# Attention tokens routed in two sets into a fixed region per expert, with slots read through a table

## What is computed

```python
t = rmsnorm(x) * rms_w
q, k, v = t @ wq, t @ wk, t @ wv                     # 8 heads of 64
attn = softmax(causal(q @ k.T * scale))
x = layernorm(x + (attn @ v * sigmoid(t @ w_gates)) @ wo)
logits = x @ Wg                                      # 16 experts
topi = top_k(logits, 2); gates = softmax over the two chosen
y = sum over the chosen e of gates[e] * ((silu(x @ W1[e] + b1[e]) * (x @ W11[e] + b11[e])) @ W2[e] + b2[e])
z = silu(x @ Ws1 + bs1) * (x @ Ws11 + bs11) @ Ws2 + bs2
out = layernorm(x + y + z)
```

## Time and profile before

| what | value |
|---|---|
| median of 3 runs | 682.15 us (680.07 to 682.47) |
| the profiled execution, its own time | 682.44 us |
| its span | 679.3 us |
| mean granted clock of TensorE | 0.965 |
| TensorE busy | 619.2 us (91%) |
| VectorE busy | 484.1 us (71%) |
| ScalarE busy | 418.7 us (62%) |
| GpSimd busy | 121.3 us (18%) |
| attention's last sum ends | 510.97 us |
| scatters run | 529.72 to 573.6 us |
| slots' matmuls start | 577.78 us |

### The profile page before, as it was taken

One profiled execution on the slowest core, in us unless ns is written; L12 is line 12 of the kernel. 1 busy time (PEld: TensorE's weight loads), 2 busy tenths in 40 slices (PEclk: granted clock), 3 DMA queues, 4 the chain that ended last, 5 costly groups with the idle time before them and its releaser, 6 DMA issues.

```text
span 679.3 us, 14812 instructions
## 1 busy us (share of the span) xinstructions
PE 619.2 (91%) x5300; PEld 509.4 (75%) x5300; DVE 484.1 (71%) x1564; ACT 418.7 (62%) x909; POOL 121.3 (18%) x243
## 2 busy tenths in 40 slices
PE   4899999999999999999999999999968898999930
PEld 2678888858888886888888688888856366999930
DVE  3788767688877677877767797776788533668736
ACT  4786556687666568765656877556664211677746
POOL 4000000002000000000000000000000676688830
PEclk9899999999999999999999999999987899899985
DMA  6520000050000005000000498000067211333242
GB/s 139 118 55 1 1 2 1 2 125 1 1 2 1 1 2 116 10 1 1 3 1 1 94 194 27 1 1 2 1 200 175 37 48 55 83 90 89 79 127 85
DMA packets 56504, 33.57 MB, mean 49 GB/s; under 512 B 23920, under 2 KB 49776, under 8 KB 56432
## 3 DMA queue, kind: packets, MB, share of 16 engines
q1 hardware_dynamic: 53872, 27.38, 19.5%
q0 software_dynamic: 2560, 5.26, 2.3%
HBM read 14.75 MB, written 9.48 MB: 36 GB/s over the span
## 4 chain that ended last, share of the span: by engine, by line
PE 68%; DVE 10%; POOL 10%; issue 6%; DMA 2%; ACT 2%; SPq 1%; DVEq 0%; POOLq 0%; ACTq 0%
PE ps_o L1079 19%; PE ps_t L966 18%; PE ps_s L1048 12%; PE ps_s L1050 10%; POOL x_sorted L466 5%; PE ps_o L1089 4%; POOL y_rows L482 4%; DVE k_l L672 3%; DVE q_hl L672 2%; PE ps_s L1199 2%; POOL row_all L473 1%; PE ps_s L974 1%; ACT k_h L501 1%; PE ps_o L1187 1%; DVE bn L707 1%
## 5 line engine op out<-in xcount | busy, mean ns | idle before, releaser
L966 PE MATMUL ps_t<-ident,probs 128*128 128x128 f32 x1104 | 173.7, 275 | 12.0 <-ACT probs L513 11.9
L966 PEld LDWEIGHTS ps_t<-ident,probs 128*128 128x128 f32 x1104 | 135.1, 141 | 48.8 <-issue 11.6
L544 ACT ACTIVATE probs<-probs,nmax 128x128 f32<-128x128 f32 (+15 forms) x128 | 153.6, 1200 | 21.2 <-DVE nmax L775 12.3
L784 DVE COPY probsT<-ps_t 128x512 f32<-128x512 f32 (+3 forms) x160 | 91.2, 570 | 101.4 <-PE ps_t L966 100.4
L555 ACT ACTIVATE probsT<-ps_t 128x512 f32<-128x512 f32 (+3 forms) x160 | 89.6, 560 | 98.7 <-PE ps_t L966 97.3
L1048 PE MATMUL ps_s<-k_h,q_hl 128*128 128x512 f32 (+3 forms) x320 | 142.3, 448 | 0.5 <-DMA k_l<-k_l 0.5
L1079 PE MATMUL ps_o<-probsT,v_sb 128*64 128x128 f32 x2176 | 140.0, 277 | 1.3 <-DVE x_acc L799 1.2
L1079 PEld LDWEIGHTS ps_o<-probsT,v_sb 128*64 128x64 f32 x2176 | 116.8, 137 | 19.6 <-issue 14.6
L770 DVE TENSOR_SCALAR_CACHE_REDUCE probs<-ps_s 128x512 f32<-128x512 f32 x192 | 128.4, 686 | 0.7
L1050 PE MATMUL ps_s<-k_l,q_hl 128*128 128x512 f32 (+3 forms) x320 | 117.0, 366 | 0.0
L438 POOL TENSOR_TENSOR rden<-rsum,gate 128x2 f32<-128x2 f32 x64 | 12.5, 195 | 402.6 <-ACT probs L544 387.4
(11 more groups left out here) (148 smaller groups left out, 706.2 us busy)
## 6 DMA issues: line engine op xcount, KB each, us to landing
k_h<-k_h SPq DMA_DIRECT2D x32, 128.0 KB, 2.3
k_l<-k_l SPq DMA_DIRECT2D x32, 128.0 KB, 2.4
w_all<-in_L_ffn_W SPq DMA_DIRECT2D x2, 2048.0 KB, 11.0
xg<-x_sorted SPq DMA_DIRECT2D x48, 64.5 KB
x_sorted<-zeros SPq DMA_DIRECT2D x12, 256.0 KB, 8.5
act_s<-y_rows SPq DMA_DIRECT2D x8, 256.0 KB, 4.8
x_acc<-in_L_attn_tokens SPq DMA_DIRECT2D x4, 256.0 KB, 3.8
out<-x_acc SPq DMA_DIRECT2D x4, 256.0 KB, 2.3
```

Of the source, the lines that this page charges most:

```text
L544: nc.scalar.activation(probs[s % 2][h][:, 0:w], probs[s % 2][h][:, 0:w], ACT.Exp, bias=nmax[:, row], scale=-1.0, accum_out=rsum[:, row]).t ...
L784: nc.vector.tensor_copy(probsT[s % 2][h][:, c * BT:c * BT + w // P, :].rearrange("p n i -> p (n i)"), ps_t[1][:, 0:w]).then_inc(moved1, 1)
L966: return nc.tensor.transpose(dst, src, ident[:, :])
```

## The change

Tokens are routed in two sets: set 0 is tiles 8 to 15 (n0, n1), set 1 is tiles 0 to 7. Each expert has a fixed region of 2048 rows in x_sorted, so that a token's row is the expert's region plus its rank, and set 0 needs no counts of set 1. x_sorted grows from 6144 to 34816 rows. A table of first rows, one for each slot tile, is made on VectorE, and SyncE reads it into registers. The end of attention has an order written out for each engine, statistics of n0 and n1 move to steps 10 and 11, the square root goes to GpSimd as a power of -0.5, gates come from tanh in place of an exponential, and the routing, norms and gates of the sets are laid between the steps of the shared expert. Tiles in SBUF are placed in another order, so that the first norms can be written while attention still runs. The cast of slot numbers moves from GpSimd to VectorE.

```diff
-    norm_at = {NT: [("stats", n0), ("stats", n1)], NT + 1: [("norm", n0), ("norm", n1), ("stats", n2)]}
+    SETS = (range(n1 * BT, (n0 + 1) * BT), range(n3 * BT, (n2 + 1) * BT))
...
+    PE_UNITS = [pair_units(False, {}),
+                ending(pair_units(True, {}),
+                       [t14a, wo12, pv13, t14b, t15a, wo13, t15b, pv14, pv15, unit("turn_x", c=n0), wo14, wo15,
+                        unit("turn_x", c=n1)])]
+    ACT_UNITS = [pair_units(False, ACT_LAG),
+                 ending(pair_units(True, ACT_LAG),
+                        [wo12, pv13, t14b, t15a, wo13, pv14, t15b, wo14, pv15, wo15, unit("turn_x", c=n0),
+                         unit("turn_x", c=n1)])]
+    DVE_UNITS = [pair_units(False, DVE_LAG),
+                 ending(ahead(ahead(pair_units(True, DVE_LAG), unit("times_wo", 10), unit("stats", c=n0)),
+                              unit("times_wo", 11), unit("stats", c=n1)),
+                        [wo12, unit("norm", c=n0), t14b, pv14, wo13, t15a, t15b, pv15, unit("norm", c=n1),
+                         unit("stats", c=n2), wo14, wo15])]
...
+            def empty_groups(groups):
+                for g in groups:
+                    sp.dma_start(view[g, :, :, 0:D], zeros[:, :].rearrange("p (n d) -> p n d", d=D)).then_inc(zfill, 16)
+
+            empty_groups(range(groups // 2))
             for p in range(PAIRS - 1):
                 for x in PE_UNITS[0]:
                     if x[:2] == ("project", K):
                         k_across(x, p * KQ_FILLS + (KQ_FILLS + high_of[x]),
                                  p * FREED + (KQ_FILLS + fill_of[x] + ONE))
-
-            sp.wait_ge(zero_set, 2)
-            view = x_sorted.rearrange("(g n p) d -> g p n d", p=P, n=BT)
-            for g in range(SLOT_TILES // BT):
-                sp.dma_start(view[g, :, :, 0:D], zeros[:, :].rearrange("p (n d) -> p n d", d=D)).then_inc(zfill, 16)
-            with nc.allow_non_contiguous_dma("one number of each row, 24 KB"):
-                sp.dma_start(x_sorted.rearrange("(n p) d -> p n d", p=P)[:, :, D].bitcast(i32),
-                             empty_row[:, :]).then_inc(zfill, 16)
+                if p == 0:
+                    empty_groups(range(groups // 2, groups))
+                if p == 1:
+                    with nc.allow_non_contiguous_dma("one number of each row, 136 KB"):
+                        for r in range(E + 1):
+                            sp.dma_start(numbers[r, :, :, D].bitcast(i32),
+                                         empty_row[:, r * REGION:(r + 1) * REGION]).then_inc(zfill, 16)
...
+            regs = [[sp.alloc_register(f"first_row{k}{i}") for i in range(IDS)] for k in range(2)]
+            first_rows = [[], []]
+
+            def load_rows(r):
+                sp.load(regs[r % 2], row_i[0:1, r * IDS:(r + 1) * IDS])
+                first_rows[r % 2][:] = [sp.snap(reg, min_val=0, max_val=SORTED - P) for reg in regs[r % 2]]
+
+            sp.wait_ge(table_ready, 1)
+            load_rows(0)
             sp.wait_ge(scattered, 16 * TOPK * NT)
             for n in range(SLOT_TILES):
+                if n % IDS == 1 and n // IDS + 1 < SLOT_TILES // IDS:
+                    load_rows(n // IDS + 1)
                 if n >= XB:
 
                     sp.wait_ge(xgT_psum, n - XB + 1)
                     sp.wait_ge(row_noted, n - XB + 1)
-                sp.dma_start(xg[:, n % XB, :], x_sorted[n * P:(n + 1) * P, :]).then_inc(xg_in[n % XB], 16)
+                at = first_rows[n // IDS % 2][n % IDS]
+                sp.dma_start(xg[:, n % XB, :], x_sorted[bass.ds(at, P), :]).then_inc(xg_in[n % XB], 16)
...
+            def row_scale(i):
+
+                cols = slice(NORM_ORDER[i] * BT, (NORM_ORDER[i] + 1) * BT)
+                pool.wait_ge(var_ready, i + 1)
+                nc.gpsimd.tensor_tensor(rstd[:, 0, cols], rstd[:, 1, cols], halves[:, cols], ALU.pow).then_inc(ln_rstd, 1)
 
             def gated_sums(p):
                 for s in range(NT):
+                    if p == PAIRS - 1 and s == NT - 1:
+                        pool.wait_ge(halves_set, 1)
+                        row_scale(0)
...
+            row_scale(1)
+            row_scale(2)
             pool.wait_ge(acc_done, ONE + PAIRS * NT)
-            nc.gpsimd.iota(rows[:, :, :, D].bitcast(i32), pattern=[[N, TOPK], [P, NT]], base=0,
-                           channel_multiplier=1).then_inc(pool_step, 1)
-
-            pool.wait_ge(pool_step, 4)
-            pool.wait_ge(zfill, 16 * (SLOT_TILES // BT + 1))
-            pool.wait_ge(rows_ready, NC)
-            pool.wait_ge(slots_ready, 1)
-            for t in range(NT):
-                nc.gpsimd.tensor_copy(slot[:, :, t], slot_f[:, :, t]).then_inc(slot_noted, 1)
-                pool.wait_ge(slot_noted, t + 1)
-                for k in range(TOPK):
-                    nc.gpsimd.indirect_dma_start(
-                        out=x_sorted, out_offset=bass.IndirectOffsetOnAxis(ap=slot[:, k, t:t + 1], axis=0),
-                        in_=rows[:, k, t, :], in_offset=None).then_inc(scattered, 16)
+            for k in range(TOPK):
+                nc.gpsimd.iota(rows[k][:, :, D].bitcast(i32), pattern=[[P, NT]], base=k * N,
+                               channel_multiplier=1).then_inc(pool_step, 1)
+
+            pool.wait_ge(pool_step, 5)
+            pool.wait_ge(zfill, 16 * (groups + E + 1))
+            for i, tiles in enumerate(SETS):
+                pool.wait_ge(rows_ready, 2 * (i + 1))
+                pool.wait_ge(slots_ready, i + 1)
+                for t in tiles:
+                    for k in range(TOPK):
+                        nc.gpsimd.indirect_dma_start(
+                            out=x_sorted, out_offset=bass.IndirectOffsetOnAxis(ap=slot[:, k, t:t + 1], axis=0),
+                            in_=rows[k][:, t, :], in_offset=None).then_inc(scattered, 16)
+                    if i == 0 and t == tiles[0]:
+                        row_scale(3)
...
+            act.preload_act_table(ACT.Silu)
+            rows_twice(n0)
+            rows_twice(n1)
...
+                if n == 1:
+                    gate_difference(0)
+                if n == 4:
+                    x_across(n2)
+                    rows_twice(n2)
+                if n == 5:
+                    x_across(n3)
+                    rows_twice(n3)
+                if n == 6:
+                    gates_across(0)
+                if n == 7:
+                    gate_difference(1)
+                if n == 13:
+                    gates_across(1)
...
+            def place(i):
+                cols = in_set(i)
+                bank = count_bank(i)
+                if i == 1:
+                    link(nc.vector.tensor_copy(counts[1][:, :, 0], before[0][:, :, HALF]))
+                dve.wait_ge(count_psum, i + 1)
+                link(nc.vector.tensor_copy(counts[i][:, :, 1:], bank[:, 3 * P:4 * P].rearrange("p (n e) -> p e n", e=E)))
+                link(nc.vector.tensor_tensor_scan(before[i][:, :, :].rearrange("p e n -> p (e n)"),
+                                                  carry[:, :, :].rearrange("p e n -> p (e n)"),
+                                                  counts[i][:, :, :].rearrange("p e n -> p (e n)"), 0.0, ALU.mult, ALU.add))
+                link(nc.vector.tensor_tensor(rank[:, cols, :], bank[:, 2 * P:3 * P].rearrange("p (n e) -> p n e", e=E),
+                                             before[i][:, :, 0:HALF].rearrange("p e n -> p n e"), ALU.add))
+                link(nc.vector.tensor_tensor(picked[:, :, cols, :], hot[:, :, cols, :],
+                                             rank[:, cols, :].unsqueeze(1).to_broadcast([P, TOPK, HALF, E]), ALU.mult))
+                link(nc.vector.tensor_reduce(slot_f[:, :, cols], picked[:, :, cols, :], X, ALU.add))
+                nc.vector.tensor_copy(slot[:, :, cols], slot_f[:, :, cols]).then_inc(slots_ready, 1)
...
+            for n in range(NC * SB):
                 shared_act(n)
...
+                if n == 0:
+                    place(0)
+                    norm("stats", n3)
+                elif n == 2:
+                    norm("norm", n2)
+                elif n == 3:
+                    norm("norm", n3)
+                elif n == 4:
+                    gates(0)
+                elif n == 5:
+                    largest_logits(1)
+                elif n == 6:
+                    choose(1)
+                elif n == 7:
+                    place(1)
+                elif n == 8:
+                    shared_add(0)
+                elif n == 9:
+                    gates(1)
+                elif n == 10:
+                    tiles_of_experts()
+                elif n == 12:
+                    shared_add(1)
+                elif n == 13:
+                    experts_of_slots()
+                elif n == 14:
+                    rows_of_slots()
+            shared_add(NC - 2)
...
+            def places(i):
+
+                tiles = SETS[i]
+                cols = slice(tiles[0] * E, (tiles[-1] + 1) * E)
```

(41 more changed lines are left out.)

269 lines of the change are left out of this document (140 added, 129 removed).

## The result

The changed kernel takes 666.02 us (median; 665.67 to 668.5) against 682.31 us (680.07 to 684.03) for the kernel before on the same chip: a ratio of 0.9747, 95% interval 0.9713 to 0.9781, 16.3 us less. The forecast was 671.8, with a range from 668.0.

What follows compares the result with a forecast made beforehand. Scatter and shared expert, ending together after attention, were taken to bound the kernel. An earlier first slot matmul (9.6 us) plus a full-clock slot loop (1.0), off the profiled 682.4, gave 671.8 us; range 668 to 677.5.

Steps and rivals of the forecast that it cites:

- What bounds the kernel: After attention, scatter and shared expert end within a microsecond; both must get faster, a shorter scatter alone brings nearly nothing.
- rival 1: At the slots' start, GpSimd's scatters or the table decide instead: slots 1.4 us later, low clock 1.0 more, 674.2; chance 0.2.
- Part 1: Attention's tail: logits read at 508.0 instead of 514.88, 6.9 us earlier, bounds 3.5 and 7.5; a GpSimd power costs 0.5.
- rival 2: Attention's tail gives half, 3.5 instead of 6.9 us, with a second low-clock stretch of 1.7: 677; chance 0.15.
- Part 2: Routing of set 0: slots at 515.0, first scatter at 515.6 against 529.72, 14 us earlier.
- the wait for act(1): Early shared expert: up(3) waits for act(1), which ends at 517.4; 3 us of idle, then one low-clock stretch.
- Part 3: Shared expert with routing laid in: up(7) ends at 532.5 against 541.9, first slot matmul at 568.2, 9.6 us earlier.
- Rival 4: VectorE's 25 us of routing inside the shared expert takes up every gain: 681; chance 0.04.
- Part 4: Scatters 1.27 us apart plus allowances for VectorE: set 1 from 538.8 to 560.6, landed 562.9, 2.4 us to spare.
- Part 5: Region per expert, 34816 rows to clear: transfers gone before k's copy at 381.6, cost 0, cover 24 us.
- rival 3: Row-number packets over 3.2 ns each delay k's copies, 730 at 172 us, or register addresses slow slots; chance 0.06.
- The loop at full clock: Slot loop: TensorE arrives after some 1.5 us of idle instead of 2.9, starts at full clock, gaining 1.0 us.

Runs made afterwards that it cites:

- the undone version: Changed kernel with TensorE and VectorE back in their old order at attention's end, first GpSimd power behind attention's last product: 668.83 us, ratio 0.9797.
- the second profile: The changed kernel measured once more with no edit: 666.7 us, ratio 0.9762, span 663.0.
- the run with everything together: Changed kernel with n3 statistics later, slot 0 weights before the last two sums, 12 + 6 extra transposes, second row-address table loaded later: 664.49 us.
- early weights: Changed kernel with slot 0's weights copied ahead of the last two shared sums, its rows transposed without waiting for the last sum: 664.33 us, ratio 0.9724.
- spare transposes: Changed kernel with six more TensorE transposes between the first two slot transposes and the first slot matmuls: 665.93 us, ratio 0.9734.

## Why the prediction was right and where it fell short

**What bounds the kernel, and the mechanism.** Right. Two paths ended together before, and both had to be shortened; the early scatters are worth 15 to 17 us (taking them back costs all of the gain), the shared expert follows, and after the change the two paths end within 2 us of each other again. Which of them ends last changes from one execution to the next: the shared expert in the first profile, as forecast, and the scatters in the second, as in rival 1, though without its loss.

**The sum, step by step**, in us of the spans; the last column is what each step added to the gap:

| step | predicted | measured | gap |
|---|---|---|---|
| first multiplication by wo (before 39.1) | 39.1 | 38.6 | -0.5 |
| from there to the logits' reading | 468.9 | 468.0 | -0.9 |
| to the start of up(3) | 9.4 | 8.5 | -0.9 |
| up(3) to the first down projection | 15.1 | 13.2 | -1.9 |
| to the shared expert's last sum | 33.6 | 32.7 | -0.9 |
| to the first slot matmul | 2.1 | 2.1 | 0 |
| loop, against 75.0 | -1.0 | -0.3 | +0.7 |
| behind the last store, against 26.5 | 0 | +0.4 | +0.4 |
| outside the span, against 3.1 | 0 | -1.4 | -1.4 |

They sum to -5.4 as they stand here and to the whole -5.6 us between 671.8 and the profiled 666.2 by unrounded marks. About 2 of the 5.6 (first line, last line) is no step of the forecast but luck in part: the mark at wo moves by 3.3 us between profiles, and the time outside the span was 1.7 to 3.7 us in the four executions.

**Part 1, the tail.** Right in place and nearly in size: the logits were read 1.4 us ahead of 508.0 at full clock, and from the mark the kernel before took 7.8 us longer to them (475.8 against 468.0). 4.1 to 6.2 of that come from the order; the rest goes with what the undone version kept, the square root that left ScalarE among it, and was not taken apart. So rival 2 is out. The price of the power on GpSimd was wrong by half (1.01 to 1.11 us against 0.5). The first one cost nothing, since it had 3 us of cover, as said; the one between the second and the third scatter made their distance 2.26 us. What the part did not say is that the low clock of the old tail can reach into the shared expert; the profiles show 0 to 4 us for that.

**Part 2 and the wait for act(1).** Slots of set 0 at 512.92 instead of 515.0, 6.4 us behind the logits where I had 7.0, so half widths on VectorE cost a little less than I took from the old rows of double width. The wait that I foresaw is there (2.29 us), and in the first profile the low clock behind it.

**Part 3, the largest miss (-1.9 and -0.9).** This is the step that failed, a mis-sized term: what is laid in between up(3) and up(7). The five up projections cost 10.6 us, low stretch included, where the forecast had 10.5. The additions cost 2.6 us where it had 4.5 (two turns 0.87 for 1.4, two sets of logits 1.62 for 2.3, the turn of the gates 0.11 for 0.4, waits 0 for 0.4). I had taken the turns and logits at their old times, but in the trace of before these lie between 510 and 520 at a granted clock of 0.74 and 0.60. The next 0.9 us are the same kind of addition: 0.7 us on top of the old 32.0, where I had 1.6. VectorE's 8 us of additions were hidden whole, as said. Rival 4, that VectorE would eat the gain, found nothing: all of TensorE's waits for act_s came to 2.7 us, under the 4 that I allowed. In the second profile there is no low stretch, and up(3) to the first down projection takes 11.5 us instead of 13.2; so whether it comes changes from one execution to the next.

**Part 4, the scatters.** Set 1 starts at 535.43 instead of 538.8, and the last one ends at 555.75 (554.79 + 0.96) instead of 560.6. Two allowances for VectorE beside them, 2 and 1.5 us, did not show: set 0 kept 1.25 to 1.27 us from its fourth scatter on, and set 1 had a mean of 1.29 over its fifteen intervals. The Trainium skill, GPSIMD Engine Reference, section 1 (Specifications), has the two engines collide when VectorE reads two inputs from SBUF. The trace agrees only in part. The longest scatter, at 553.17, took 1.31 us, 1.65 at 550.16 in the run with everything together, 1.71 before, against 0.96, and each of these started within half a microsecond behind the start of a 0.93 or 0.94-us operation of the table on two such inputs. But a scatter that had started ahead of such an operation (549.38, the operation at 549.77) kept its 0.96, and in the run with the scatters taken back the longest (1.32 at 562.61) ran beside a copy of weights, which has one input. One or two such scatters of 32 are a cost of 0.4 to 1 us. The path behind the last scatter was longer than I took it, 5.9 to 6.2 us from its start to the first slot matmul instead of 5.2. So the cover was about 2 us in the first profile, where I gave 2.4, and none in the second. Rival 1 decides as soon as the shared expert gains 2 us more.

**Part 5, the region.** Right. The 17 transfers of row numbers were issued from 270.8 and gone by about 325 (DMA share 1.19 in 280 to 320), 56 us ahead of k's next copy, which stood at 381.0 (before 381.6):

```profile
x_sorted<-empty_row SPq DMA_DIRECT2D x17, 8.0 KB, 11.8
...
L435 SPq DMA_DIRECT2D xg<-x_sorted x48: 332/333/870, 557.4 to 623.6; - x48
```

34816 packets of 4 bytes in 54 us are 1.6 ns each, half of what rival 3 needed. A slot's rows are issued in 333 ns (before 320), though the load of the next eight addresses stands between the first two, and the second rows land 1.3 us after the first (559.37, 560.69) instead of 0.7. SyncE had the table 1.0 us before the scatters were through.

**The loop at full clock.** Wrong: I counted on 1.5 us of idle and a loop at full clock. The idle was 0.78 + 0.87 us in two pieces from 560.83, and the clock was 0.50 at 564. It was worth more than the 1.0. It came with early weights, with spare transposes and with the old tail, not in the two profiles of the changed kernel.

**The range.** Its lower end took a better tail and no low stretch, 3.6 us. It left out that the durations of turns and logits had been read at the low clock, which errs to one side in each of them, and the 1.5 us or more by which two executions differ.

## What to carry to other kernels

Two paths that end together have to be shortened together, and after that they have to be measured for cover again: here 3 us off one of them was worth nothing. Durations read in a stretch at the low clock must be scaled before they are moved into one at full clock, and an order without idle time on TensorE is worth its waits and, at times, the clock behind them. A stretch where two paths end within 2 us should be profiled twice before one of them is named. Transfers that GpSimd issues one by one should start as soon as any part of their input is known.
